# A vision tower with a mixture of experts on one core: the shared expert's down product in three products of rounded high and low parts

## The reference, cut to what matters

```python
h = tok(x)                                   # 64 images: 38 tokens of 256 channels
h = h + attn(layernorm(h))                   # gated attention with a decay, 4 heads of 128
h = h + ffn(layernorm(h))

def swiglu(x, gw, uw, dw):
    return silu(x @ gw) * (x @ uw) @ dw

def ffn(x):                                  # x: 2432 rows of 256
    shared = swiglu(x, shared_gate_w, shared_up_w, shared_down_w)      # 256 -> 512 -> 256
    ids, scores = argmax(x @ gate_w), sigmoid(max(x @ gate_w))
    routed = one of 32 experts for each row, on x * score
    return shared + routed
```

## Time and profile before

| | |
|---|---|
| median of 3 runs | 649.88 us (649.38 to 652.09) |
| the profiled execution's own time | 654.7 us |
| its span | 652.9 us |
| mean granted TensorE clock | 0.988 of full |
| TensorE busy | 607.6 us, 93% |
| VectorE busy | 429.5 us, 66% |
| ScalarE busy | 375.2 us, 57% |
| GpSimd busy | 197.4 us, 30% |

### The profile page before, as it was taken

How to read it: one execution, slowest core, us unless ns; L and a number is a source line. 1 busy time by engine, 2 the same in 40 slices (tenths; PEclk the granted TensorE clock), 3 DMA queues, 4 the chain that set the end, 5 groups by cost and what they waited for, 6 DMA issues and landing times.

```text
span 652.9 us, 10636 instructions
## 1 busy us (share of the span) xinstructions
PE 607.6 (93%) x3615; PEld 510.1 (78%) x3615; DVE 429.5 (66%) x1338; ACT 375.2 (57%) x839; POOL 197.4 (30%) x226
## 2 busy tenths in 40 slices
PE   4899899999998998999999998988999999999995
PEld 3688778878878878878878977766788888888884
DVE  1644785865856865866765866675876777776672
ACT  1328668449439529539538758243666666666661
POOL 5100110231232133133033233353256662232451
PEclk9999899999999999999998999899999999999999
DMA  8339410030030030030010011185999999999960
GB/s 291 132 85 369 122 56 1 20 94 21 20 95 21 20 94 21 19 95 21 8 51 20 2 37 37 35 303 169 392 391 378 379 348 350 373 369 404 343 214 23
DMA packets 44597, 101.56 MB, mean 156 GB/s; under 512 B 9295, under 2 KB 30589, under 8 KB 39672
## 3 DMA queue, kind: packets, MB, share of 16 engines
q1 hardware_dynamic: 35280, 89.07, 38.1%
q0 software_dynamic: 7696, 8.49, 4.7%
q10 hardware_dynamic: 1560, 3.23, 1.5%
HBM read 80.17 MB, written 23.32 MB: 159 GB/s over the span
## 4 chain that ended last, share of the span: by engine, by line
PE 71%; ACT 14%; DVE 8%; issue 2%; POOL 1%; DMA 1%; SPq 0%; DVEq 0%; ACTq 0%; POOLq 0%
PE bank L2253 16%; PE bank L1390 11%; PE bank L2272 9%; PE bank L1355 8%; PE bank L1512 4%; PE bank L1490 3%; PE bank L1455 3%; PE bank L2261 2%; PE bank L1416 2%; PE bank L1572 2%; PE bank L1364 2%; ACT v L505 2%; ACT hst L581 2%; ACT L596 1%; ACT L592 1%
## 5 line engine op out<-in xcount | busy, mean ns | idle before, releaser
L456 POOL TENSOR_TENSOR rstd_h<-var_h,minus_half 114x4 f32<-114x4 f32 (+1 forms) x24 | 24.3, 1014 | 173.3 <-DVE var_h L999 173.3
L2077 POOL DMA_INDIRECT out<-rows,bg x32 | 37.6, 1175 | 82.4 <-DVE rows L2143 81.1
L1355 PE MATMUL bank<-patch,lin_w 128*128 128x288 f32 x192 | 52.6, 428 | 8.7 <-DMA col_t<-cols 7.9
L2253 PE MATMUL bank<-w_hi,x_hi 128*128 128x512 f32 x148 | 56.5, 463 | 2.7 <-DVE x_lo L2155 2.7
L1355 PEld LDWEIGHTS bank<-patch,lin_w 128*128 128x128 f32 x192 | 37.4, 201 | 20.6 <-DMA col_t<-cols 7.9
L898 DVE SCALAR_TENSOR_TENSOR y<-xm,conv_t,y 128x296 f32<-128x296 f32 (+2 forms) x96 | 43.7, 512 | 6.2 <-ACT xm L505 6.2
L2253 PE MATMUL bank<-w_lo,x_hi 128*128 128x512 f32 x148 | 46.3, 394 | 0.0
L2253 PE MATMUL bank<-w_hi,x_lo 128*128 128x512 f32 x148 | 46.2, 393 | 0.0
L2179 DVE TENSOR_TENSOR act_e<-silu_e,bank 128x512 f32<-128x512 f32 x37 | 25.5, 688 | 31.0 <-PE bank L2253 30.3
L2149 DVE TENSOR_TENSOR w_lo<-wts,w_hi 128x1024 fp32r<-128x1024 f32 x36 | 43.1, 1217 | 0.5 <-ACT w_hi L2201 0.5
L2228 ACT ACTIVATE silu_e<-bank 128x512 f32<-128x512 f32 x37 | 22.1, 598 | 35.2 <-PE bank L2253 35.2
(11 more groups left out here) (261 smaller groups left out, 1658.8 us busy)
## 6 DMA issues: line engine op xcount, KB each, us to landing
wts<-w_exp SPq DMA_DIRECT2D x18, 1024.0 KB
x_act<-w_exp SPq DMA_DIRECT2D x10, 1024.0 KB
silu_z<-w_exp SPq DMA_DIRECT2D x9, 1024.0 KB
wts_down<-w_exp SPq DMA_DIRECT2D x18, 512.0 KB
patch<-patches SPq DMA_DIRECT2D x8, 864.0 KB, 6.0
down_w<-w_exp SPq DMA_DIRECT2D x10, 512.0 KB
lin_w<-w_exp SPq DMA_DIRECT2D x9, 512.0 KB
b_zone_dram<-act_t SPq DMA_DIRECT2D x1, 4160.0 KB, 28.4
```

Source lines behind the costliest of these rows:

```text
L1355: last = pe.matmul(fb[c][:, 0:GS * N], lin_w[:, k, c * 128:(c + 1) * 128], patch[:, k, :], start=(k == 0), stop=(k == KF - 1))
L2077: pool.indirect_dma_start(out, bass.IndirectOffsetOnAxis(ap=rows_at, axis=0), rows[:, k % 4, :], None, bounds_check=T - 1, oob_is_err=Fals ...
L2253: last = pe.matmul(banks[2 + 2 * e + u][:, :], x[:, e, c * SLOT:(c + 1) * SLOT], w[:, e, u, c * I:(c + 1) * I], start=(n == 0), stop=(n == ...
```

## The change

It splits the two factors of `shared_down` and multiplies three times in float32r. Each of the 64 float32 matmuls (8 groups, 2 halves, 4 values of k) becomes three float32r matmuls. `sd_hi` and `sd_lo` are made once, in `split_shared`. For each group ScalarE rounds the four `act_t[:, k]` into `act_hi`, and VectorE subtracts them into `act_lo`; these calls stand at chosen places of the steps and of the three stretches behind them. `sgu_raw` now shares its memory with `act_hi` and `act_lo`, so the first `act_hi` waits for the last subtraction of `split_shared`. Apart from this, two semaphores are merged into others (`s_fln` into `s_fexp`, `s_last` into `s_hn`); each wait still waits for the same instructions.

```diff
+        sd_hi = sb("sd_hi", [128, KI, D], f32r)
+        sd_lo = sb("sd_lo", [128, KI, D], f32r)
+        with nc.sbuf_tensor("sgu_raw", [128, KD, 2 * I], f32) as sgu_raw:
+            pass
+        act_hi = sb("act_hi", [128, KI, GT], f32r)
+        act_lo = sb("act_lo", [128, KI, GT], f32r)
...
@@ scalar: split_shared, then the new call
                 copy(route_w[:, :, 0:E], route_raw).then_inc(s_split, 1)
+                copy(sd_hi[:], sd_w[:]).then_inc(s_split, 1)
...
+            def act_hi_of(m, k):
+                act.wait_ge(s_act, KI * m.n + k + 1)
+                wait(act, s_sd_mm, KD * m.n)
+                if m.n == 0 and k == 0:
+                    act.wait_ge(s_prep, 26)
+                copy(act_hi[:, k, :], act_t[:, k, :]).then_inc(s_act_hi, 1)
...
@@ scalar: next_last
             silu_g_of(m, 2)
+            act_hi_of(m, 0)
+            act_hi_of(m, 1)
             silu_g_of(m, 3)
+            act_hi_of(m, 2)
+            act_hi_of(m, 3)
             score_rows(m)
...
@@ vector: split_shared, then the new call
+                dve.wait_ge(s_split, 6)
+                dve.tensor_tensor(sd_lo[:], sd_w[:], sd_hi[:].bitcast(f32), ALU.subtract).then_inc(s_prep, 1)
...
+            def act_lo_of(m, k):
+                dve.wait_ge(s_act_hi, KI * m.n + k + 1)
+                dve.tensor_tensor(act_lo[:, k, :], act_t[:, k, :], act_hi[:, k, :].bitcast(f32),
+                                  ALU.subtract).then_inc(s_act_lo, 1)
...
@@ vector: near
+            act_lo_of(m, 0)
+            act_lo_of(m, 1)
             expert_act(m, 3)
             h2_of(a)
+            act_lo_of(m, 2)
+            act_lo_of(m, 3)
             mixed_gates(f)
...
@@ tensor
             def shared_down(m, halves=range(KD)):
                 pe.wait_ge(s_act, KI * m.n + KI)
                 for c in halves:
+                    half = slice(c * 128, (c + 1) * 128)
                     for k in range(KI):
-                        last = pe.matmul(mb[c][:, 0:GT], sd_w[:, k, c * 128:(c + 1) * 128], act_t[:, k, :],
-                                         start=(k == 0), stop=(k == KI - 1))
+                        pe.wait_ge(s_act_hi, KI * m.n + k + 1)
+                        for w in (sd_hi, sd_lo):
+                            pe.matmul(mb[c][:, 0:GT], w[:, k, half], act_hi[:, k, :],
+                                      start=(k == 0 and w is sd_hi), stop=False)
+                    for k in range(KI):
+                        pe.wait_ge(s_act_lo, KI * m.n + k + 1)
+                        last = pe.matmul(mb[c][:, 0:GT], sd_hi[:, k, half], act_lo[:, k, :],
+                                         start=False, stop=(k == KI - 1))
                     last.then_inc(s_sd_mm, 1)
```

More of the change, by code:

```diff
@@ L75, in groups_phase @@
         up_lo = sb("up_lo", [128, KD, 2 * INNER], f32r)
-        sgu_raw = sb("sgu_raw", [128, KD, 2 * I])
         patch = sb("patch", [128, KF, GS * N])
@@ L226, in groups_phase @@
         s_fexp = sem("s_fexp")
-        s_fln = sem("s_fln")
         s_logf = sem("s_logf")
@@ L254, in groups_phase @@
         s_sq = sem("s_sq")
-        s_last = sem("s_last")
         s_hn = sem("s_hn")
@@ L293, in groups_phase @@
         s_act = sem("s_act")
+        s_act_hi = sem("s_act_hi")
+        s_act_lo = sem("s_act_lo")
         s_sd_mm = sem("s_sd_mm")
@@ L332, in by_dve @@
         def by_dve(n):
-            return n
+            return (NT + 1) * n
         @block.sync
@@ L594, in log_f @@
             def log_f(a):
-                act.wait_ge(s_fexp, a.n + 1)
-                act.activation(fln[:], fexp[:], ACT.Ln, bias=1.0).then_inc(s_fln, 1)
+                act.wait_ge(s_fexp, 2 * a.n + 1)
+                act.activation(fln[:], fexp[:], ACT.Ln, bias=1.0).then_inc(s_fexp, 1)
             def decay(a, j):
@@ L688, in step @@
                 if f: silu_z_of(f, 1)
-                if m: silu_g_of(m, 3)
+                if m:
+                    act_hi_of(m, 0)
+                    act_hi_of(m, 1)
+                    silu_g_of(m, 3)
                 if f and f.n != 1: x_act_of(f, 1)
-                if m: score_rows(m)
+                if m:
+                    act_hi_of(m, 2)
+                    score_rows(m)
+                    act_hi_of(m, 3)
                 if a: head_norm(a, 0)
@@ L921, in log_f @@
             def log_f(a):
-                dve.wait_ge(s_fln, a.n + 1)
+                dve.wait_ge(s_fexp, 2 * a.n + 2)
                 dve.scalar_tensor_tensor(logf[:], gl[:, :, NH:], 0.0, fln[:], ALU.min,
@@ L1005, in last_channel @@
                 dve.scalar_tensor_tensor(o[0:n, j, :, LAST], mv_h[0:n, j, :, 0], -float(LAST), rstd_h[0:n, j, :],
-                                         ALU.mult, ALU.mult).then_inc(s_last, 1)
+                                         ALU.mult, ALU.mult).then_inc(s_hn, 1)
             def head_norm(a, j):
@@ L1167, in step @@
                 if a: norm_2(a, 0)
-                if m: expert_act(m, 3)
+                if m:
+                    expert_act(m, 3)
+                    act_lo_of(m, 0)
+                    act_lo_of(m, 1)
+                    act_lo_of(m, 2)
                 if a:
@@ L1171, in step @@
                     head_var(a, 0)
+                if m: act_lo_of(m, 3)
+                if a:
                     head_stats(a, 1)
@@ L1496, in heads_t @@
                 pe.wait_ge(s_hn, by_dve(a.n + 1))
-                pe.wait_ge(s_last, NT * (a.n + 1))
                 for j in range(NT):
```

## The result

The changed kernel is **slower**. The first comparison gave 664.55 us as the median of 4 executions against 649.65 us before, a ratio of 1.0226 (95% interval 1.0188 to 1.0265): 14.9 us, with 660.2 forecast and 654 to 666 as the range. A second comparison, with more executions of both kernels, gave 663.82 against 650.66, a ratio of 1.0181 (1.0133 to 1.0229): 13.2 us between the medians. The ratio is an estimate of its own and not the quotient of the two medians (1.0202 here); by it the second comparison gives 11.8 us. The profiled execution took 664.56 us with a span of 662.7; that is 9.8 us above the span before, where the sum had 10.3. Why the medians lie further apart than the traces is the first question of the experiments.

The account below looks back on a forecast made before the run. TensorE is busiest (93%), but VectorE, only about 0.4 us ahead at heads_t, was taken to set the step. Terms 6.0 + 1.1 + 0.5 - 0.2 + 1.5 - 0.3 + 1.7 = +10.3 us on 649.9 give 660.2, range 654 to 666.

Parts of the forecast that it names:

- the sum: Whole kernel: the terms of all places added, +10.3 us on a profiled execution of 654.7 us.
- The sign: Whole kernel: the change makes it slower, chance 0.87.
- the mechanism: Regular steps: subtractions delay VectorE's head statistics, thus silu_z and heads_t, against a margin of 0.4 us.
- the last group: Last group before the experts: act_hi, w_hi, w_lo and subtractions delay the product's end and ffn_rows, +1.7 us.
- near: Group ending beside the last projection: late low part +0.5 us, other half -0.2.
- next to last: Next to last group: four subtractions ahead of VectorE's second mix delay down, +1.5 us; second product half -0.3.
- The regular step: Five steps holding the product: heads_t released later by VectorE and TensorE, +1.2 us each, +6.0 in all.
- the lock: Each step: rstd_h waits for the fourth act_lo on a shared port pair, 0.3 us, +1.5, 661.7; chance 0.05.
- The product: Shared product on TensorE: 3.45 us a group, a gain of 0.7 us where nothing makes it wait.
- Weight split: End of the third step, once: making sd_hi (0.95 us) and sd_lo (1.15) is not hidden, +1.1 us.
- rival 3: Steps: added waits make the clock fall more often, 662 to 663 us, or 668 if in all five; chance 0.2.
- The differences carry over: From profile to median: the profiled execution is 4.8 us above the median 649.88, so 649.9 + 10.3 = 660.2.

Follow-up runs that it names:

- v1: Changed kernel with the five steps reordered to give VectorE room, float32 product in the three groups behind, weight split in idle time: 649.95 us beside 651.30, ratio 0.9972.
- v3: v2 with the high parts of both halves ahead of all low parts in the five steps: 649.50 us beside 650.66, ratio 0.9958.
- cost_only: Changed kernel with all new parts still made, but TensorE multiplying in plain float32: 666.39 us beside 652.60, ratio 1.0193.
- gain_only: Changed kernel without the four subtractions of each group, third product reading act_hi instead of act_lo: 654.56 us beside 652.60, ratio 1.0028.
- v0: Control for v1: same order, float32 product everywhere, no parts: 651.06 us beside 651.30, ratio 0.9981.
- after_again: The changed kernel, unchanged, in more executions and profiled a second time: 663.82 us beside 650.66, ratio 1.0181.
- four_first: Changed kernel with the fourth act_hi ahead of xs_rows and the fourth act_lo ahead of the first head statistics: 674.39 us beside 651.30, ratio 1.0324.
- v0b: v0 with head_var moved behind the last act_t: 653.57 us beside 650.71, ratio 1.0033.
- v2: v1 with the first head_var behind the last act_t and the new product also in the three groups behind the steps: 649.61 us beside 650.71, ratio 0.9963.

## Why the prediction was right, and where not

The sign, the mechanism and the order of size were right; the measured difference is 3 to 5 us above the forecast (1.5 to 4.4 by the ratios), and the time is inside the range. That the two spans lie 9.8 us apart, so near the sum of 10.3, is in part luck: the steps and the last group cost 2.3 us more than forecast, and near, the next to last group and the experts 3.1 less, of which 1.6 are a fall of the clock in the kernel before and 1.1 the experts, whose difference did not repeat.

- **The regular step** (forecast +1.2, five times +6.0): the places and their order came out as forecast (embedding half 5.80 us behind the product, forecast 5.7; heads_t released by both sides within 0.2 us of each other). Measured +1.33, and +7.0 with the late fourth product. The term missed is the 0.16 us that rstd_h takes longer beside the fourth subtraction. The prediction had called the lock a rival, since a small tensor_tensor of VectorE ran beside rstd_h at its usual 0.16 us (and rstd_h at its usual 1.01). That operation starts inside rstd_h, where v1's full-size subtractions slow nothing either; the fourth act_lo starts ahead of it. So the row could not decide the question. The rival's price, 0.3 us, was too high and the forecast's, none, too low.
- **The product** gained what was forecast where nobody is waited for (v3: 24 multiplies in 3.34 us, forecast 3.45), and nothing in the steps of the changed kernel: cost_only and gain_only show that.
- **Weight split**: +1.14 for +1.1, with sd_hi at 1.05 us and sd_lo at 1.21.
- **near**: +0.3 forecast. The table's -1.12 holds a half-clock stretch of the execution before (353.18 to 358.35, 5.17 us; after 3.58, 1.59 less); without it +0.47. The fall stands in both profiled executions of the kernel before and in neither of the changed kernel; v0, which has the float32 product too, has none and takes 64.71 us, 1.6 less. So nothing shows that the change removes it.
- **next to last** (+1.5 and -0.3): measured +1.01 up to down and -0.37 behind it. VectorE's 1.6 us were spent, but TensorE's wait for act_t ahead of them shrank from 2.23 us to 1.70, which the prediction took as unchanged.
- **The last group** (+1.7): measured +3.02. The working's own last step has a slip (445.1 + 1.8 is 446.9, not 447.1, so +1.5). The timeline of TensorE after:

```profile
452.64 1.00 PE L1634 MATMUL bank<-act_lo,sd_hi 128*128 128x304 f32 x2 [1.43 <-DVE act_lo L1154]
453.44 0.46 PE L1630 MATMUL bank<-act_hi,sd_hi 128*128 128x304 f32 x1
...
456.38 0.36 PE L1972 MATMUL bank<-ident,slot_e 114*1 114x114 f32 x2
```

  The wait is the one forecast; behind it the clock is at half, and the second half of the product takes 2.94 us (453.44 to 456.38) where its 12 multiplies take 1.77 by the forecast's prices. That is 1.2 of the 1.3 us missed: rival 3, the clock, in one place. The fall stands there in both profiled executions of the changed kernel (granted clock 0.50 from 452.0 to 455.3 us in after_again) and in neither of the kernel before. four_first has the same wait of 1.43 us at this place and no fall behind it, and its last group takes 18.07 us, 1.27 less.
- **"The differences carry over"** from the profiled execution to the median is the step that failed most. The execution before was at a clock of 0.988, and times like the median's 649.88 belong to 0.993 or more, while the changed kernel shows 0.991 at most and 0.988 in five of ten executions. At equal clock the difference is 10 to 11.5 us, the sum within its error; the rest of the 14.9 is the clock, in part chance in the few executions, in part (1 to 3 us over all executions) a clock that falls more often in the changed kernel. That its added waits cause this is not shown: the fall in the last group speaks for it, and so do two of the five long waits of four_first, but most of the falls of four_first stand elsewhere, and no run changed the waits alone. Rival 3 is therefore partly true, and not in the steps, where the three separate waits brought no fall in either profiled execution of the changed kernel.

## What to carry to other kernels

Before work is moved from the busiest engine to another, follow who releases it around the place: here VectorE was 66% busy and 0.4 us ahead where it counts, and 1.2 us of its work cost a step 1.3 us while TensorE's gain vanished in a wait. Make room on the engine that receives the work first (here 1.8 us of convolution moved to where VectorE idled for 3.3), then the same product is worth 0.64 us a step against its control in the same order (v0 to v1), and 0.33 in a better order, where the next wait takes the rest (v0b to v2). Price a faster instruction against the best order without it, too. And compare one execution's trace with a median only at the same granted clock.

## What the runs showed of the hardware

- The granted clock differs from one execution of a kernel to the next, and the time with it: 649.8 us at 0.993 or more, 656.5 at 0.987 or less. One place in the group near takes 37.6, 39.2 or 42.4 us for nearly the same work, behind the same four waits of 0.24 to 0.51 us.
- One wait of TensorE of 2.43 us in each step (four_first) went with a lower clock, 0.970 to 0.978, than waits of 0.46, 0.69 and 0.53 us in its place, 0.982 to 0.991. The clock fell behind two of its five long waits, and behind none of the five triples in either profiled execution of the changed kernel.
- The power operation of GpSimd on 114x4 takes 1.20 us instead of 1.04 when a VectorE subtraction of two SBUF operands starts 0.17 us ahead of it and ends 0.30 us after its start. Beside a VectorE multiplication with one operand in PSUM at the same place it takes 1.04 (v0, v1), and beside subtractions that start 0.22 us or more behind it too, which are not slowed themselves (v1).
- Over 128x304, a float32 product of 128x128 takes 0.52 us from start to next start and three float32r products 0.42; a group of eight takes 4.15 and 3.34 us (v0b, v3).
- VectorE's act_lo lasts 0.47 us in the records and the next operation starts 0.39 behind its start, in the kernels read here (three in 1.16 us from start to next start); for ScalarE's act_hi it is 0.44 and 0.35.
